# Solving the diagonal blocks of two neighbouring tiles together in the delta-rule stage of a fused transformer kernel, with a new order of stages and 16 buffer slots

## The chip, the cores and the metric

The program runs on one core of a Trainium2 chip. The time is the device time of one execution in microseconds (us); the profile's engines are PE (matrix multiply; PEld its weight loads), DVE, ACT, POOL and SP, which only issues transfers here. The time before is the median of three runs.

## What is computed

Four sub-layers, each followed by a layer norm, on 16 sequences of 1024 tokens of 256 features. The first two (a causal linear attention with an MLP, and a quantised linear layer) and the convolutions in front of the third are phases A and B of the kernel, the fourth (a mixture of experts on the first 1024 tokens) is phase D. The change is in phase C, the delta rule of the third sub-layer and what is made of its output:

```python
def step(S, xs):                       # one chunk, per head
    qi, ki, ui, wi = xs
    attn = jnp.where(tri_lo, qi @ jnp.swapaxes(ki, -1, -2), 0.0)
    u_i = ui - wi @ S
    o = qi @ S + attn @ u_i
    return (S + jnp.swapaxes(ki, -1, -2) @ u_i, o)
...
stats = jnp.concatenate([_stats(local_short), _stats(local_long), _stats(delta_out), _stats(vh)], -1)
...
hgate = jax.nn.gelu(gate_in @ mlp_w1 + mlp_b1, approximate=False)
logits = hgate @ mlp_w2 + mlp_b2
probs = jax.nn.softmax(logits / temp, -1)
...
o = probs[..., 0:1] * local_short + probs[..., 1:2] * local_long + probs[..., 2:3] * delta_out + probs[..., 3:4] * vh
o = o * jax.lax.rsqrt(jnp.mean(o * o, -1, keepdims=True) + 1e-05) * rms_w
return o.reshape(b, l, H * DV) @ Wo
```

There are 4 heads of 64 features; a layer norm and the residual follow.

## The kernel before

Phase C works on 128 tiles of 128 tokens. A "lane" `s` is one of the 16 sequences, `i` one of its 8 tiles; the tiles are taken lane by lane, so that a tile's state `S` comes from 16 tiles earlier. Each tile passes through some 20 stages, which are spread over the engines and pipelined over the tiles. The table `starts` gives for each engine and stage a time within one tile's passage; `interleaved` sorts stage and lane by `s * PERIOD + start`, and this is the order in which each engine issues its stages. The times of the table set the order alone: at run time an engine goes through its own list and waits at semaphores. PERIOD is the table's distance of two tiles. All 128 tiles are written out one after another.

The recurrence inside a tile is solved in 4 blocks of 32 tokens. PE writes `k @ S` and the values into a bank (`kS`); then for each block b ACT takes the 32 rows out as `z`, PE multiplies them with the ready-made 32x32 inverse (`solve{b}`, 4 heads, each a matmul of 32 rows with 64 columns), ACT takes them out as `u`, and PE adds what the solved blocks contribute to the next (`carry{b}`). Block b lies on partitions 32b to 32b+31, for operands and result alike, so a `solve{b}` works in row group b of the array. Neighbouring tiles use two different banks (`CHAIN`). An fp32 matmul shows as two passes in the profile, so a `solve` is 8 passes.

After the blocks PE makes the output (`o`) and the state's increment (`dS`); DVE takes statistics of four sources (`stats`, the longest stage there), POOL takes powers (`l2`, `softmax`), PE runs the gate (`base`, `statsT`, `pre`, `logits`, `turn_logits`), ACT, DVE and POOL mix the sources, PE projects (`oT`, `Wo`), and two layer norms follow (`lnC`, `lnD`), whose variance goes over POOL. DVE and POOL both start their part of `mix` when DVE has signalled `coef_ready`. SP issues the loads of a tile (8 and 3 transfers, `load` and `load_src`) and the store of its result. Each buffer of `slots(...)` exists SLOTS times, or as often as its own number says.

Of the kernel before, what the change touches and what calls it, by code (L numbers as in the profile page):

```python
# [30 lines left out]
CUT = 32  # L31
# [1414 lines left out]
def phase_c(nc, w, k, scratch, out, batches, banks):  # L1446
# [15 lines left out]
    BLOCKS = P // CUT  # L1462
# [2 lines left out]


    starts = {
        "sp": {"load": 0.00, "load_src": 0.51, "lnD": 99.59},
        "pe": {"gram": 5.48, "kS": 6.66, "solve0": 8.45, "carry1": 9.84, "solve1": 11.99, "carry2": 14.89,
               "solve2": 16.30, "carry3": 17.79, "solve3": 20.45, "o": 23.27, "dS": 34.76, "base": 41.20,  # L1470
               "statsT": 48.10, "pre": 51.20, "logits": 55.51, "turn_logits": 59.66, "oT": 76.15, "Wo": 78.51},
        "act": {"kS": 7.84, "solve0": 9.25, "carry1": 11.38, "solve1": 12.79, "carry2": 15.69, "solve2": 17.20,
                "carry3": 18.59, "solve3": 22.47, "o": 26.00, "base": 44.73, "statsT": 48.58, "pre": 52.82,
                "logits": 56.89, "mix": 67.63, "rms": 71.70, "oT": 76.77, "lnC": 94.92, "lnD": 98.78},
        "dve": {"gram": 6.66, "dS": 35.49, "stats": 35.92, "logits": 60.13, "softmax": 66.78, "mix": 67.42,
                "add": 69.04, "rms": 72.39, "Wo": 80.67, "lnC_stats": 81.10, "lnD_stats": 95.84},
        "pool": {"l2": 42.93, "softmax": 62.47, "mix": 67.41, "rms": 73.12, "lnC_stats": 91.17, "lnD_stats": 97.45},
    }
    run = partial(run_pipelined, written=WRITTEN)
    order = {eng: interleaved(own, STEPS, PERIOD) for eng, own in starts.items()}  # L1480
# [3 lines left out]
    CHAINS = 2  # L1484
    CHAIN = [BANKS - C - CHAINS + m for m in range(CHAINS)]
# [12 lines left out]
    with ExitStack() as ctx:  # L1498
        def sb(name, shape):
            return ctx.enter_context(nc.sbuf_tensor("c_" + name, shape, F32))  # L1500

        def slots(name, shape, n=SLOTS):


            own = [sb(f"{name}{m}", shape) for m in range(n)]
            return [own[m % n] for m in range(SLOTS)]

# [3 lines left out]
        psum = [ctx.enter_context(nc.psum_tensor(f"c_bank{b}", [P, BANK], F32)) for b in range(BANKS)]  # L1511
# [23 lines left out]
        z = slots("z", [P, H, DH], 2)  # L1535
# [22 lines left out]
        oT, xs = xT, o_sb  # L1558
# [23 lines left out]
        with nc.Block() as block:  # L1582
# [66 lines left out]
        chain_full, z_ready, u_ready = ([sem(f"{n}{m}") for m in range(CHAINS)] for n in (  # L1649
            "chain_full", "z_ready", "u_ready"))  # L1650
# [220 lines left out]
        def _(dve):  # L1871
# [16 lines left out]
            def stats_stage(i, s):  # L1888

                sl = s % SLOTS  # L1890
                in_sbuf(dve, i, s, "o")
                dve.wait_ge(src_in[s % SRCS], 48 * (uses(i, s, SRCS) + 1))
                for n in range(SRC):
                    for h in range(H):
                        ins = dve.bn_stats(bn[sl][:, n * H + h], src[sl][:, n, h * DH:(h + 1) * DH])  # L1895
                link(ins)
                b = bn[sl][:].rearrange("p (s h) e -> p s h e", s=SRC)
                out_ = stats[sl][:, :, 0].rearrange("p h s e -> p s h e")
                mean, diff, m2, total = (stat[n][:] for n in ("mean", "diff", "m2", "abs"))
# [3 lines left out]
                link(dve.tensor_reduce(total, src[sl][:].rearrange("p s (h d) -> p s h d", h=H), AX.X, ALU.add,  # L1903
                                       apply_absolute_value=True))
# [3 lines left out]
                dve.tensor_scalar(out_[:, :, :, 2], total, 1.0 / DH, None, ALU.mult)  # L1908
                link(dve.scalar_tensor_tensor(m2, diff, DH / 4.0, m2, ALU.mult, ALU.add))
                dve.tensor_scalar(out_[:, :, :, 1], m2, 1.0 / DH, None, ALU.mult)  # L1910
                dve.scalar_tensor_tensor(l2sq[sl][:].rearrange("p (s h) -> p s h", s=SRC), mean, DH / 4.0, m2,  # L1911
                                         ALU.mult, ALU.add).then_inc(N["l2sq_ready"], 1)

            def logits(i, s):
                sl = s % SLOTS
                src_ = full(dve, i, s, "logits")
                ins = dve.scalar_tensor_tensor(logit[sl][:], heads(src_[:, 0:P])[:, :, 0:SRC], inv_temp[:, 0:1],
                                               gate_b2[:, None, :].broadcast_to([P, H, SRC]), ALU.mult, ALU.add)
                done_with(ins, s, "logits")
                in_sbuf(dve, i, s, "logits")  # L1920
                link(dve.tensor_reduce(small[:], logit[sl][:], AX.X, ALU.max))
                dve.tensor_tensor(logit[sl][:], logit[sl][:], small[:, :, None].broadcast_to([P, H, SRC]),  # L1922
                                  ALU.subtract).then_inc(N["logit_ready"], 1)

            def softmax(i, s):
                sl = s % SLOTS
                dve.wait_ge(N["exp_ready"], seq(i, s))
                link(dve.tensor_reduce(small[:], expd[sl][:], AX.X, ALU.add))
                link(dve.reciprocal(small[:], small[:]))
                link(dve.tensor_tensor(coef[sl][:], expd[sl][:], small[:, :, None].broadcast_to([P, H, SRC]), ALU.mult))  # L1930
# [29 lines left out]
            def norm_stats(which, src_, var_sem, ready=None):  # L1960
# [19 lines left out]
        def _(pe):  # L1980
# [25 lines left out]
            def k_state(i, s):  # L2006
# [10 lines left out]
                                    stop=True, skip_group_check=True)  # L2017
                ins.then_inc(chain_full[m], 1)

            def solve(b):  # L2020

                def stage(i, s):
                    m, sl, rows = s % CHAINS, s % SLOTS, slice(b * CUT, (b + 1) * CUT)
                    pe.wait_ge(z_ready[m], BLOCKS * uses(i, s, CHAINS) + b + 1)
                    for h in range(H):
                        ins = pe.matmul(psum[CHAIN[m]][rows, D + h * DH:D + (h + 1) * DH], inverse[sl][rows, h], z[sl][rows, h],  # L2026
                                        start=True, stop=True, skip_group_check=True)
                    ins.then_inc(chain_full[m], 1)
# [305 lines left out]
```

## Time and profile before

| | |
|---|---|
| median of 3 runs | 5204.71 us (5199.36 to 5206.39) |
| profiled execution: its time | 5198.8 us |
| profiled execution: its span, first to last instruction | 5197.0 us |
| mean granted clock | 0.957 |
| PE busy | 4769.5 us (92%) |
| DVE busy | 4121.5 us (79%) |
| ACT busy | 2835.2 us (55%) |
| POOL busy | 2775.8 us (53%) |

Phase C is the part from about 3370 to 5056 us of the span. The busy shares are of the whole span; what an engine has left in phase C must be read from that stretch. All times below are us from the start of the span.

### The profile page before, as it was taken

Reading aid. Unit: us, or ns where it says so; the run is one execution under the profiler, and the core shown is the slowest. Engines: PE = TensorE matmul, PEld = TensorE weight load, DVE = VectorE, ACT = ScalarE, POOL = GpSimd, SP = SyncE. Lnnn points to the kernel's source line nnn. Section 1 sums busy time; section 2 is a strip of 40 time slices with the busy share of each in tenths; the row PEclk is TensorE's granted clock in tenths of the full one; section 3 lists DMA queues with packets and bytes.
Section 4 is the critical chain, followed back from the end, with each engine's and each line's share of the span. In section 5 each row is a group of like instructions: output and inputs, shape, how many; then the busy total and the mean of one; then the engine's idle time right before and its main releaser. Section 6 shows DMA issues by size and latency. Waiting matters only on the chain. (4 is left out here: it accounts for less than half of the span.)

```text
span 5197.0 us, 116254 instructions
## 1 busy us (share of the span) xinstructions
PE 4769.5 (92%) x42012; PEld 3991.7 (77%) x42012; DVE 4121.5 (79%) x12689; ACT 2835.2 (55%) x6469; POOL 2775.8 (53%) x3719
## 2 busy tenths in 40 slices
PE   5999999999999999999999849699999999999968
PEld 4887887878787788778878649678888888888855
DVE  4778988988988898898889842168988889888861
ACT  2554555555455555545555412157777777777751
POOL 1344444444443444444444323248888888888870
PEclk9999999999999999999999969889999999999979
DMA  1121221122122112212121238633433343333320
GB/s 43 42 61 52 63 61 57 53 63 65 50 61 63 54 56 65 64 47 65 57 59 57 61 78 199 165 105 109 115 114 108 114 115 109 112 114 113 110 66 33
DMA packets 738174, 416.01 MB, mean 80 GB/s; under 512 B 341764, under 2 KB 725576, under 8 KB 737608
## 3 DMA queue, kind: packets, MB, share of 16 engines
q1 hardware_dynamic: 667144, 372.92, 25.2%
q10 hardware_dynamic: 65664, 16.78, 1.4%
q0 software_dynamic: 4800, 18.88, 1.2%
q8 instruction: 342, 5.60, 0.5%
q14 instruction: 224, 1.84, 0.1%
HBM read 220.98 MB, written 187.43 MB: 79 GB/s over the span
## 5 line engine op out<-in xcount | busy, mean ns | idle before, releaser
L636 POOL TENSOR_TENSOR a_shift<-a_mean_var,a_eps 128x2 f32<-128x2 f32 x256 | 71.7, 280 | 1423.8 <-DVE a_mean_var L918 1423.8
L932 DVE SCALAR_TENSOR_TENSOR a_cv<-a_raw,a_taps,a_cv 128x256 f32<-128x256 f32 x1152 | 567.2, 565 | 10.1 <-DVE a_scaled L864 9.9
L1151 PE MATMUL a_bank<-a_turned,a_w 128*128 128x256 f32 x2048 | 456.8, 381 | 4.8 <-ACT a_turned L719 4.8
L1053 PE MATMUL a_bank<-a_w,a_hidden 128*128 128x256 f32 x2048 | 452.8, 379 | 0.9 <-ACT a_hidden L764 0.9
L1151 PEld LDWEIGHTS a_bank<-a_turned,a_w 128*128 128x128 f32 x2048 | 384.6, 190 | 59.3 <-ACT a_turned L719 8.8
L1053 PEld LDWEIGHTS a_bank<-a_w,a_hidden 128*128 128x128 f32 x2048 | 384.1, 190 | 51.2 <-ACT a_hidden L764 1.7
L1737 POOL TENSOR_TENSOR c_stats<-c_l2sq,half 128x16 f32<-128x16 f32 x128 | 374.7, 2927 | 57.6 <-DVE c_l2sq L1911 57.6
L1744 POOL TENSOR_TENSOR c_expd<-c_e,c_logit 128x16 f32<-128x16 f32 x128 | 371.3, 2901 | 5.7 <-DVE c_logit L1922 5.7
L897 DVE TENSOR_TENSOR a_masked<-a_bank,keep_causal 128x512 f32<-128x512 f32 x512 | 317.5, 682 | 61.2 <-PE a_bank L1109 59.8
L2026 PE MATMUL c_bank<-c_z,c_inverse 32*32 32x64 f32 x4096 | 323.9, 218 | 4.1 <-ACT c_z L1786 4.0
L2026 PEld LDWEIGHTS c_bank<-c_z,c_inverse 32*32 32x32 f32 x4096 | 241.1, 105 | 72.0 <-issue 20.6
L780 ACT ACTIVATE a_raw<-a_bank 128x512 f32<-128x512 f32 x192 | 114.9, 598 | 301.9 <-PE a_bank L1044 301.9
L667 POOL TENSOR_TENSOR a_coef<-a_base,a_powers_half 128x24 f32<-128x24 f32 x64 | 274.9, 4295 | 5.0
L1895 DVE BATCH_NORM_STATS2 c_bn<-c_src 128x6 f32<-128x64 f32 x2048 | 272.0, 211 | 4.0
L792 ACT ACT_TABLE_LOAD x62 | 79.5, 1283 | 334.5 <-PE a_bank L1171 334.5
L2041 PEld LDWEIGHTS c_bank<-c_u,c_grams 32*32 32x32 f32 (+2 forms) x3072 | 182.6, 107 | 95.3 <-issue 70.0
L982 DVE TENSOR_TENSOR a_T<-a_T,a_product 128x30 f32<-128x30 f32 (+14 forms) x480 | 242.3, 505 | 16.5
L2041 PE MATMUL c_bank<-c_u,c_grams 32*32 32x64 f32 (+2 forms) x3072 | 241.8, 220 | 9.0 <-ACT c_u L1783 4.8
L1786 ACT ACTIVATE c_z<-c_bank 32x256 f32<-32x256 f32 x512 | 191.7, 374 | 93.4 <-PE c_bank L2041 58.9
L1754 POOL TENSOR_TENSOR c_mixed<-c_src,c_coef 128x256 f32<-128x256 f32 x256 | 176.4, 710 | 113.0 <-DVEq L1932 113.0
L1430 PE MATMUL b_bank<-b_window,b_matrix 128*128 128x128 f32 x1024 | 226.0, 397 | 9.7 <-POOL b_window L1322 9.7
L1430 PEld LDWEIGHTS b_bank<-b_window,b_matrix 128*128 128x128 f32 x1024 | 211.5, 211 | 23.1 <-issue 10.2
(291 smaller groups left out, 13254.3 us busy)
## 6 DMA issues: line engine op xcount, KB each, us to landing
a_x<-in_x SPq DMA_DIRECT2D x64, 256.0 KB, 3.0
scratch_xb<-a_xb SPq DMA_DIRECT2D x64, 256.0 KB, 2.1
scratch_xbT<-a_turned SPq DMA_DIRECT2D x128, 128.0 KB, 2.2
scratch_qT<-a_cv SPq DMA_DIRECT2D x128, 128.0 KB, 2.2
scratch_v<-a_qkv_rows SPq DMA_DIRECT2D x64, 256.0 KB, 2.2
scratch_kn<-a_kn SPq DMA_DIRECT2D x64, 256.0 KB, 2.1
scratch_vb<-a_qkv_rows SPq DMA_DIRECT2D x64, 256.0 KB, 2.1
scratch_kT<-a_kT SPq DMA_DIRECT2D x128, 128.0 KB, 2.6
```

The source lines that it names most:

```text
L667: link(pool.tensor_tensor(coef[s][:], base[s][:], powers_half[:], ALU.pow))
L897: ins = dve.tensor_tensor(masked[t][:, r], src[:].rearrange("p (h i) -> p h i", h=C * 2), k["keep_causal"][:, None, :].broadcast_to([P, C ...
L932: ins = dve.scalar_tensor_tensor(cv[s][:, n, c], raw[s][:, n, c, j:j + TOK], taps[:, n, c, j:j + 1], cv[s][:, n, c], ALU.mult, ALU.add)
L982: ins = dve.tensor_tensor(rest, rest, part, ALU.add)
L1053: ins = pe.matmul(dst[:, t * D:(t + 1) * D], src[s][:, c, tile_cols(t)], weight[:, c], start=(c == 0), stop=(c == chunks - 1))
L1151: ins = pe.matmul(dst[:, at:at + TOK], w1_sb[:, c, m * P:(m + 1) * P], x1nT[s][:, c], start=(c == 0), stop=(c == C - 1))
L1430: ins = pe.matmul(dst[:, (c - q * QUAD) * N:(c - q * QUAD + 1) * N], taps_of, window[h][:, :, c], start=True, stop=True)
L1737: pool.tensor_tensor(stats[s % SLOTS][:, :, 0, :, 3], l2sq[s % SLOTS][:].rearrange("p (s h) -> p h s", s=SRC), k["half"][:].rearrange("p ( ...
L1744: pool.tensor_tensor(expd[sl][:], e_base[:].rearrange("p (h e) -> p h e", h=H), logit[sl][:], ALU.pow).then_inc(N["exp_ready"], 1)
L1895: ins = dve.bn_stats(bn[sl][:, n * H + h], src[sl][:, n, h * DH:(h + 1) * DH])
L2026: ins = pe.matmul(psum[CHAIN[m]][rows, D + h * DH:D + (h + 1) * DH], inverse[sl][rows, h], z[sl][rows, h], start=True, stop=True, skip_gro ...
L2041: ins = pe.matmul(psum[CHAIN[m]][rows, h * DH:(h + 1) * DH], grams[sl][known, h % 2, h // 2, 0, rows], u_sb[sl][known, h], start=False, st ...
```

## The change

`solve{b}` for b of 0 and 1 now issues block b of its own tile and block b+2 of the tile before, head by head in turn. `solve2` and `solve3` issue nothing but for the last tile. The table of starts is new, with PERIOD 11.70 in place of 12.90, and DVE's `gram` stands at 6.77 in place of 6.66, and SLOTS is 16 in place of 8 (buffers with a number of their own keep it). DVE's scratch tile `small` is split in two, `largest` and `total`.

```diff
-    SLOTS = 8
-    PERIOD = 12.90
+    SLOTS = 16
+    PERIOD = 11.70
...
-        "pe": {"gram": 5.48, "kS": 6.66, "solve0": 8.45, "carry1": 9.84, "solve1": 11.99, "carry2": 14.89,
...
-        "pool": {"l2": 42.93, "softmax": 62.47, "mix": 67.41, "rms": 73.12, "lnC_stats": 91.17, "lnD_stats": 97.45},
...
+        "pe": {"gram": 5.48, "kS": 6.65, "solve0": 8.93, "carry1": 11.35, "solve1": 13.49, "carry2": 15.69,
...
+        "pool": {"l2": 39.42, "softmax": 68.60, "mix": 78.84, "rms": 94.91, "lnC_stats": 112.54,
+                 "lnD_stats": 120.14},
...
-        small = sb("small", [P, H])
+        largest, total = sb("largest", [P, H]), sb("total", [P, H])
...
+            def solve_one(b, i, s, h):
+
+                m, sl, rows = s % CHAINS, s % SLOTS, slice(b * CUT, (b + 1) * CUT)
+                ins = pe.matmul(psum[CHAIN[m]][rows, D + h * DH:D + (h + 1) * DH], inverse[sl][rows, h], z[sl][rows, h],
+                                start=True, stop=True, skip_group_check=True)
+                if h == H - 1:
+                    ins.then_inc(chain_full[m], 1)
+
             def solve(b):
 
                 def stage(i, s):
-                    m, sl, rows = s % CHAINS, s % SLOTS, slice(b * CUT, (b + 1) * CUT)
-                    pe.wait_ge(z_ready[m], BLOCKS * uses(i, s, CHAINS) + b + 1)
+                    both = [(b, i, s)]
+                    if s > 0:
+                        both.append((b + 2, i, s - 1))
+                    elif i > 0:
+                        both.append((b + 2, i - 1, STEPS - 1))
+                    for b_, i_, s_ in both:
+                        pe.wait_ge(z_ready[s_ % CHAINS], BLOCKS * uses(i_, s_, CHAINS) + b_ + 1)
                     for h in range(H):
-                        ins = pe.matmul(psum[CHAIN[m]][rows, D + h * DH:D + (h + 1) * DH], inverse[sl][rows, h], z[sl][rows, h],
-                                        start=True, stop=True, skip_group_check=True)
-                    ins.then_inc(chain_full[m], 1)
+                        for b_, i_, s_ in both:
+                            solve_one(b_, i_, s_, h)
                 return stage
```

On PE, one tile's period in the middle of phase C, before. `c_z,c_inverse` is a solve, `c_u,c_grams` with 32x64 a carry; x4 are the four heads.

```order
L2001 MATMUL c_bank<-c_qkT 128x256 x4
L2014 MATMUL c_bank<-c_vb,ident 128x256
L2016 MATMUL c_bank<-c_state,c_qkT 128x128 x2
L2026 MATMUL c_bank<-c_z,c_inverse 32x64 x4
L2108 MATMUL c_bank<-ident,c_logitsT 128x128
L2026 MATMUL c_bank<-c_z,c_inverse 32x64 x4
L2063 MATMUL c_bank<-c_u,c_kn 128x128 x2
L2070 MATMUL c_bank<-ident,c_stats 128x128
L2041 MATMUL c_bank<-c_u,c_grams 32x64 x4
L2052 MATMUL c_bank<-c_state,c_qkT 128x128 x2
L2055 MATMUL c_bank<-c_u,c_grams 128x64 x4
```

The same place on PE in the changed kernel, from the same matmuls on:

```order
L2002 MATMUL c_bank<-c_qkT 128x256 x4
L2015 MATMUL c_bank<-c_vb,ident 128x256
L2017 MATMUL c_bank<-c_state,c_qkT 128x128 x2
L2074 MATMUL c_bank<-c_state,c_qkT 128x128 x2
L2077 MATMUL c_bank<-c_u,c_grams 128x64 x4
L2024 MATMUL c_bank<-c_z,c_inverse 32x64 x8
L2085 MATMUL c_bank<-c_u,c_kn 128x128 x2
L2092 MATMUL c_bank<-ident,c_stats 128x128
L2124 MATMUL c_bank<-c_pre,c_gate 32x128 x8
L2136 MATMUL c_bank<-ident,c_on 128x128 x2
L2063 MATMUL c_bank<-c_u,c_grams 32x64 x8
```

The four solves of a period, x4 each, have become two of x8, and the two carries between them stand side by side (x8). `o` (`c_state,c_qkT` and `c_u,c_grams` with 128x64) now stands between `kS` and the solve.

Inside one x8 on PE in the changed kernel, with buffer numbers: bank 4 is the younger tile's (block 0), bank 5 the older one's (block 2).

```order
L2077 MATMUL c_bank1<-c_u0,c_grams0 128x64 x4
L2024 MATMUL c_bank4<-c_z0,c_inverse2 32x64
L2024 MATMUL c_bank5<-c_z1,c_inverse1 32x64
...
L2085 MATMUL c_bank2<-c_u0,c_kn0 128x128 x2
L2063 MATMUL c_bank4<-c_u2,c_grams2 32x64 x4
L2063 MATMUL c_bank5<-c_u1,c_grams1 32x64 x4
```

The two rows in the middle come four times in turn; each tile keeps its bank.

On ACT in the changed kernel, behind the take-out of `z` after `kS`: the square of the mix, `lnC` (which waits for POOL's variance), the output's four heads, and then the two take-outs of `u` that the solve pair left.

```order
L1787 ACTIVATE c_z<-c_bank 32x256
L1815 ACTIVATE c_mixed<-c_o 128x256
L1826 ACTIVATE c_xc<-c_o,c_shift,c_rstd 128x256
L1796 ACTIVATE c_src<-c_bank,c_coef_in 128x64 x4
L1784 ACTIVATE c_u<-c_bank 32x256 x2
L1860 ACTIVATE c_statsT<-c_bank 128x128
L1851 ACTIVATE c_logitsT<-c_bank 128x128
```

The place on ACT before where two take-outs of `u` follow each other, behind the output's norm `lnD` (`c_y`):

```order
L1786 ACTIVATE c_z<-c_bank 32x256
L1825 ACTIVATE c_y<-c_xc,c_shift,c_rstd 128x256
L1783 ACTIVATE c_u<-c_bank 32x256 x2
L1859 ACTIVATE c_statsT<-c_bank 128x128
L1786 ACTIVATE c_z<-c_bank 32x256
L1854 ACTIVATE c_xT<-c_bank,c_rms_w 128x256
```

In both a norm that waits for POOL stands ahead of two take-outs of `u`, for which PE's next carry waits: before it is `lnD`, now `lnC`, and now the output's four heads stand between them too.

## Rows read from the trace of the kernel before

**Rows 1.** The page's head: engines over the whole span.

```profile
PE 4769.5 (92%) x42012; PEld 3991.7 (77%) x42012; DVE 4121.5 (79%) x12689; ACT 2835.2 (55%) x6469; POOL 2775.8 (53%) x3719
```

**Rows 2.** Engines by stretch in phase C; the columns are named in the first line.

```profile
core 0: us, PE busy (x) PEld busy (x) DVE busy (x) ACT busy (x) POOL busy (x), PEclk, DMA share, GB/s
...
4000.00:4200.00 200.00, 199.44 (x2132) 160.71 (x2132) 179.59 (x764) 150.06 (x413) 175.89 (x241) 1.00 0.39 112
```

**Rows 3.** Timeline of PE, one tile's period: start, length, passes.

```profile
4005.86 1.16 PE L2091 MATMUL c_bank<-c_statsT,c_gate_stats 64*128 64x128 f32 x16
4006.95 1.13 PE L2120 MATMUL c_bank<-c_Wo,c_xT 128*128 128x256 f32 x4
...
4008.57 1.16 PE L2078 MATMUL c_bank<-c_xT,c_gate 128*128 128x128 f32 x8
4009.66 0.63 PE L2026 MATMUL c_bank<-c_z,c_inverse 32*32 32x64 f32 x8
4010.22 0.64 PE L2102 MATMUL c_bank<-c_pre,c_gate 128*32 128x128 f32 x16
```

**Rows 4.** Timeline of PE in phase A: four row groups in turn, and blocks of 32 columns.

```profile
2003.69 1.15 PE L1109 MATMUL a_bank<-a_phiq_own,a_phik 32*128 32x256 f32 x16
2023.76 0.76 PE L1200 MATMUL a_bank<-a_kT 64*32 64x32 f32 x64 [0.77 <-ACT a_kT L817]
```

**Rows 5.** Waits of all engines from 3600 to 4800: us in total, times, longest.

```profile
POOL c_mixed L1754 <- DVEq L1932: 82.8, 95, 1.0
DVE c_state L1885 <- PE c_bank L2063: 51.4, 95, 0.6
```

**Rows 6.** All of line 1937: DVE's part of the mix, ns min/median/max.

```profile
L1937 DVE TENSOR_TENSOR c_mixed<-c_src,c_coef x128: 425/892/895, 3442.0 to 5039.4; 128x256 f32<-128x256 f32 x128
```

**Rows 7.** Timeline of DVE in one period.

```profile
4002.92 0.58 DVE L1885 TENSOR_TENSOR c_state<-c_state,c_bank 64x128 f32<-64x128 f32 x2 [0.55 <-PE c_bank L2063]
...
4008.06 0.16 DVE L1928 TENSOR_REDUCE c_small<-c_expd 128x4 f32<-128x16 f32 x1
...
4008.99 0.89 DVE L1937 TENSOR_TENSOR c_mixed<-c_src,c_coef 128x256 f32<-128x256 f32 x1
4009.92 0.42 DVE L1957 TENSOR_TENSOR c_o<-c_bank,c_xb 128x256 f32<-128x256 f32 x1
```

**Rows 8.** Timeline of POOL and ACT in the same period.

```profile
4000.67 0.18 POOL L1729 TENSOR_TENSOR c_shift<-c_mean_var,c_eps 128x1 f32<-128x1 f32 x1
4001.97 0.20 POOL L1761 TENSOR_TENSOR c_o_ssq<-c_o_ssq,c_eps 128x4 f32<-128x4 f32 x1
...
4008.98 1.38 POOL L1754 TENSOR_TENSOR c_mixed<-c_src,c_coef 128x256 f32<-128x256 f32 x2 [0.79 <-DVEq L1932]
4010.32 2.93 POOL L1737 TENSOR_TENSOR c_stats<-c_l2sq,half 128x16 f32<-128x16 f32 x1
...
4002.56 0.76 ACT L1783 ACTIVATE c_u<-c_bank 32x256 f32<-32x256 f32 x2
...
4006.36 0.93 ACT L1795 ACTIVATE c_src<-c_bank,c_coef_in 128x64 f32<-128x64 f32 x4
```

**Rows 9.** Timeline of phase C's start: DVE's first, second and seventh `gram`, one PE carry.

```profile
3380.95 1.29 DVE L1876 TENSOR_TENSOR c_grams<-c_bank,c_keep 128x512 f32<-128x512 f32 x2 [8.67 <-PE c_bank L2001]
...
3384.99 1.03 PE L2041 MATMUL c_bank<-c_u,c_grams 32*32 32x64 f32 x8 [0.55 <-ACT c_u L1783]
...
3394.14 1.29 DVE L1876 TENSOR_TENSOR c_grams<-c_bank,c_keep 128x512 f32<-128x512 f32 x2 [11.91 <-PE c_bank L2001]
...
3457.75 1.29 DVE L1876 TENSOR_TENSOR c_grams<-c_bank,c_keep 128x512 f32<-128x512 f32 x2 [0.29 <-PE c_bank L2001]
```

**Rows 10.** Timeline of DVE at phase C's end, from its last `gram`.

```profile
4983.39 1.25 DVE L1876 TENSOR_TENSOR c_grams<-c_bank,c_keep 128x512 f32<-128x512 f32 x2
...
5027.41 0.17 DVE L1928 TENSOR_REDUCE c_small<-c_expd 128x4 f32<-128x16 f32 x1 [5.67 <-POOL c_expd L1744]
...
5055.07 0.18 DVE L1966 BATCH_NORM_AGGREGATE c_mean_var<-c_bn_ln 128x2 f32<-128x6 f32 x1
```

More of the change, by code:

```diff
@@ L1467, in phase_c @@
     starts = {
-        "sp": {"load": 0.00, "load_src": 0.51, "lnD": 99.59},
-        "pe": {"gram": 5.48, "kS": 6.66, "solve0": 8.45, "carry1": 9.84, "solve1": 11.99, "carry2": 14.89,
[L1470 to L1476, printed above, removed]
-        "pool": {"l2": 42.93, "softmax": 62.47, "mix": 67.41, "rms": 73.12, "lnC_stats": 91.17, "lnD_stats": 97.45},
+        "sp": {"load": 0.00, "load_src": 0.51, "lnD": 122.92},
+        "pe": {"gram": 5.48, "kS": 6.65, "solve0": 8.93, "carry1": 11.35, "solve1": 13.49, "carry2": 15.69,
+               "solve2": 20.63, "carry3": 23.59, "solve3": 25.19, "o": 30.94, "dS": 32.92, "base": 39.60,
+               "statsT": 45.06, "pre": 49.18, "logits": 56.94, "turn_logits": 59.19, "oT": 104.59, "Wo": 106.18},
+        "act": {"kS": 7.83, "solve0": 10.76, "carry1": 12.18, "solve1": 14.30, "carry2": 17.73, "solve2": 22.14,
+                "carry3": 24.38, "solve3": 26.31, "o": 32.79, "base": 41.48, "statsT": 46.18, "pre": 50.79,
+                "logits": 58.08, "mix": 83.23, "rms": 90.07, "oT": 105.21, "lnC": 113.85, "lnD": 122.11},
+        "dve": {"gram": 6.77, "dS": 33.65, "stats": 34.08, "logits": 62.54, "softmax": 78.20, "mix": 78.65,
+                "add": 86.62, "rms": 90.70, "Wo": 111.03, "lnC_stats": 111.38, "lnD_stats": 114.68},
+        "pool": {"l2": 39.42, "softmax": 68.60, "mix": 78.84, "rms": 94.91, "lnC_stats": 112.54,
+                 "lnD_stats": 120.14},
     }
@@ L1898, in stats_stage @@
                 out_ = stats[sl][:, :, 0].rearrange("p h s e -> p s h e")
-                mean, diff, m2, total = (stat[n][:] for n in ("mean", "diff", "m2", "abs"))
+                mean, diff, m2, sizes = (stat[n][:] for n in ("mean", "diff", "m2", "abs"))
                 dve.tensor_tensor(mean, b[:, :, :, 1], b[:, :, :, 4], ALU.add)
@@ L1902, in stats_stage @@
                 dve.tensor_tensor(m2, b[:, :, :, 2], b[:, :, :, 5], ALU.add)
-                link(dve.tensor_reduce(total, src[sl][:].rearrange("p s (h d) -> p s h d", h=H), AX.X, ALU.add,
+                link(dve.tensor_reduce(sizes, src[sl][:].rearrange("p s (h d) -> p s h d", h=H), AX.X, ALU.add,
                                        apply_absolute_value=True))
@@ L1907, in stats_stage @@
                 dve.tensor_tensor(mean, mean, mean, ALU.mult)
-                dve.tensor_scalar(out_[:, :, :, 2], total, 1.0 / DH, None, ALU.mult)
+                dve.tensor_scalar(out_[:, :, :, 2], sizes, 1.0 / DH, None, ALU.mult)
                 link(dve.scalar_tensor_tensor(m2, diff, DH / 4.0, m2, ALU.mult, ALU.add))
@@ L1920, in logits @@
                 in_sbuf(dve, i, s, "logits")
-                link(dve.tensor_reduce(small[:], logit[sl][:], AX.X, ALU.max))
-                dve.tensor_tensor(logit[sl][:], logit[sl][:], small[:, :, None].broadcast_to([P, H, SRC]),
+                link(dve.tensor_reduce(largest[:], logit[sl][:], AX.X, ALU.max))
+                dve.tensor_tensor(logit[sl][:], logit[sl][:], largest[:, :, None].broadcast_to([P, H, SRC]),
                                   ALU.subtract).then_inc(N["logit_ready"], 1)
@@ L1927, in softmax @@
                 dve.wait_ge(N["exp_ready"], seq(i, s))
-                link(dve.tensor_reduce(small[:], expd[sl][:], AX.X, ALU.add))
-                link(dve.reciprocal(small[:], small[:]))
-                link(dve.tensor_tensor(coef[sl][:], expd[sl][:], small[:, :, None].broadcast_to([P, H, SRC]), ALU.mult))
+                link(dve.tensor_reduce(total[:], expd[sl][:], AX.X, ALU.add))
+                link(dve.reciprocal(total[:], total[:]))
+                link(dve.tensor_tensor(coef[sl][:], expd[sl][:], total[:, :, None].broadcast_to([P, H, SRC]), ALU.mult))
                 link(dve.scalar_tensor_tensor(coef[sl][:], coef[sl][:], 1.0 - 2.0 * FLOOR, floor[:], ALU.mult, ALU.add))
@@ L2018, in k_state, with solve_last, stage @@
                 ins.then_inc(chain_full[m], 1)
+            def solve_one(b, i, s, h):
[4 more added lines that the diff above has]
+                    ins.then_inc(chain_full[m], 1)
             def solve(b):
                 def stage(i, s):
-                    m, sl, rows = s % CHAINS, s % SLOTS, slice(b * CUT, (b + 1) * CUT)
-                    pe.wait_ge(z_ready[m], BLOCKS * uses(i, s, CHAINS) + b + 1)
-                    for h in range(H):
-                        ins = pe.matmul(psum[CHAIN[m]][rows, D + h * DH:D + (h + 1) * DH], inverse[sl][rows, h], z[sl][rows, h],
-                                        start=True, stop=True, skip_group_check=True)
-                    ins.then_inc(chain_full[m], 1)
+                    both = [(b, i, s)]
[5 more added lines that the diff above has]
+                        pe.wait_ge(z_ready[s_ % CHAINS], BLOCKS * uses(i_, s_, CHAINS) + b_ + 1)
+                    for h in range(H):
+                        for b_, i_, s_ in both:
+                            solve_one(b_, i_, s_, h)
+                return stage
+            def solve_last(b):
+                def stage(i, s):
+                    if i == TILES - 1 and s == STEPS - 1:
+                        pe.wait_ge(z_ready[s % CHAINS], BLOCKS * uses(i, s, CHAINS) + b + 1)
+                        for h in range(H):
+                            solve_one(b, i, s, h)
                 return stage
@@ L2128, in _ @@
                           stop=True).then_inc(N["pre_opened"], 1)
-            for b in range(BLOCKS):
+            for b in range(2):
                 stages[f"solve{b}"] = solve(b)
+                stages[f"solve{b + 2}"] = solve_last(b + 2)
             for b in range(1, BLOCKS):
```

## The prediction

> **What bounds the kernel now.** I read the page's head first [rows 1]: PE is busy 92% of the whole span, but DVE 79% is an average over phases with other limits. So I went on to the engines by stretch in the middle of phase C [rows 2]: there PE is busy 199.44 of 200 us at the full clock (1.00, the 2.4 GHz level), DVE 90% and POOL 88%. The list of waits over 1200 us of this stretch [rows 5] has no row of PE. PE never waits: phase C goes at PE's pace. The reader is to see in the same list how little the others have left. DVE waits 51.4 us in 95 tiles, 0.54 per tile, always for PE's state increment; POOL waits 82.8 us, 0.87 per tile, always for DVE's `coef_ready`.
>
> The period: DVE's seventh `gram` starts at 3457.75 [rows 9], its last, the 128th, at 4983.39 [rows 10]. 1525.64 us over 121 tiles is 12.61 us per tile. So DVE needs 12.61 - 0.54 = 12.07 us per tile when it waits for nobody, POOL 12.61 - 0.87 = 11.74.
>
> **The solves.** A `solve` of 8 passes takes 4010.22 - 4009.66 = 0.56 us [rows 3], 70 ns a pass, four of them 2.24 us per tile. All passes of one solve use one row group. What alternation of row groups does is seen twice. `pre` (L2091, two halves of 64 rows in turn) issues 16 passes of 128 columns in 1.09 us, 68 ns each; `base` (L2078, all 128 rows), with as many columns, takes 1.09 us for 8, 136 ns each [rows 3]. Half, as two row groups should give. In phase A, 16 passes of 256 columns over four row groups take 1.15 us, 72 ns each [rows 4], where L2120 with all rows takes 1.13 for 4 [rows 3]: a quarter. The pair of solves works in row groups b and b+2, writes different partitions and different banks. So I take half: 35 ns a pass, 0.56 us for the 16 passes of a pair. The bounds are 70 ns (nothing overlaps, 1.12 us) and the 12 ns a pass of L1200's 64 passes in 0.76 us [rows 4] (0.19 us). PE saves 2 x 0.56 = 1.12 us per tile and needs 11.49. The carries, 8 passes each, keep their cost.
>
> A rule of the Trainium skill speaks against this (TensorE: Matmul & The Clock Gate, "Back-to-back issue gap"): with the hardware decoder off, a matmul costs its sequencer about 62 ns however small it is. By it a pair would cost 0.99 us, PE 12.35 and the kernel about 5173 us by the sum below, an estimate; the trace's 12 ns a pass [rows 4] contradicts it for this program.
>
> **Where the gain ends.** PE at 11.49 is faster than DVE at 12.07, so DVE takes over the period: of PE's 1.12 us only 0.54 are worth anything. DVE's instructions are the same ones in another order; splitting `small` changes none of them and removes no semaphore, and 16 slots only relax waits that have no row in [rows 5]. I price both at nothing. If a slot wait had mattered it would stand as a wait on SP's loads ahead of PE's `gram`; the load leads `gram` by 5.5 us in the table before and after.
>
> DVE's part of the mix has a median of 892 ns, a minimum of 425 [rows 6]. It starts with POOL's mix (4008.99 and 4008.98 [rows 7, 8]), because both wait for the same signal. POOL will still get there early: its 11.74 against 12.07 leaves 0.33 us, and all of it lies at that wait. So the 892 stay in DVE's 12.07.
>
> **Does the new order make DVE wait elsewhere?** I lay one period out, zero where DVE ends `stats`. DVE then does `logits`, `add`, `Wo`, `lnC_stats`, `gram`, `softmax` (0.93 us), `mix` (0.93), `rms`, `lnD_stats`, `dS` and `stats` (5.14 from `dS`'s start to `stats`' end) [rows 7]. That leaves 5.07 for the seven short ones; less 1.2 for `gram` and an estimated 1.1 for `rms` and `lnD_stats`, the first four take 2.8. The tightest path: POOL's `l2` 2.9 (start at most 0.3), its `lnC` 1.30 [rows 8] to 4.5; ACT's norm, no longer than the 0.93 of the output, to 5.4; the output 0.93 to 6.4; two `u` 0.76 [rows 8] to 7.1. Behind it on PE wait the two carries and then, up to the end of the next `gram`, an estimated 6.8 of PE's 11.49: 13.9. DVE wants that `gram` at 12.07 + 2.8 = 14.9. One microsecond is to spare. DVE's `stats` wants the output at 7.5 and has it at 6.4. `dS` leaves PE about 3.6 us behind PE's `gram`, and DVE wants it about 4.1 behind its own start of `gram`. No new DVE wait, by some margin.
>
> **Start and end of phase C.** At the start PE goes hop by hop: 1.03 us of passes and about 0.5 waiting for ACT [rows 9]. Between the first two `gram` (13.19 us) lie six hops, in the new order four: 10.2. Later intervals carry both tiles' solves in the same four hops; I take 66 us for the first six against 76.8 before (3457.75 - 3380.95), -11, bounds 0 and -20. At the end, from the last `gram` 71.9 us pass [rows 10]. POOL's last stage stood 7.0 periods behind `gram` in the table and stands 9.7 behind now, so more is still open when the last tile enters. By the tables POOL has one more power of the softmax (2.9), two mixes (1.34), two of `rms` (an estimated 1.9) and five norms (1.3) to do: 16 us. Against that, DVE waits 5.67 us at such a power there, which the new table sets further apart. I take +12, bounds 0 and +24.
>
> **Sum.** 121 x -0.54 = -65; -11; +12: -64. The profiled execution took 5198.8 us, which gives 5135; the median of the runs lies 5.9 above the profiled one, so 5140.
>
> **The rivals.**
> - *DVE's mix escapes POOL's* (0.12). DVE drops towards 12.07 - 0.47 and POOL's 11.74 becomes the period: another 0.33 x 121 = 40, 5100 us. The minimum of 425 [rows 6] shows that it can; the same wait for both engines speaks against it. The Trainium skill (SBUF — State Buffer, "Who interferes with whom") has the two-input DVE instruction and POOL's reads exclude each other, first come first served, so the gain hangs on DVE coming first.
> - *New short waits of DVE*, or solve pairs that overlap only partly (0.13): `gram`, `dS` and the norm are set close behind their sources in the table. 0.25 us a tile costs 30: 5170. The 62 ns rule falls in here; the trace gives it 0.02 of these.
> - *The pair does not overlap* (0.05): PE stays at 12.61 without a gap, start and end cancel: 5205. [rows 3, 4] speak against it.
> - *Slower* (0.09): ACT's `lnC` waits for POOL, and behind it on ACT stand the output and both `u`, for which PE's carries wait. The path above would have to be 1.5 us longer than laid out (1.0 to spare and the 0.54) before the period passes 12.61; 2 us longer gives 13.1 and 121 x 0.46 = 56 more than before: 5260. The path is pinned by POOL, which is busy 11.74 of 12.07, and this speaks for it.
> - *As forecast* (0.61): its own range is 5120 to 5160, from the bounds of start and end and the scatter of the runs.
>
> **How the numbers follow.** The range takes in the forecast, the escape and the short waits, and leaves out no overlap and slower: 5100 to 5180. A measurement of this kernel tells about 0.2% (10 us) from no change. Faster: 0.61 + 0.12 + 0.13 = 0.86; the same: 0.05; slower: 0.09.
>
> **What would show it.** The changed trace should have 16 solve passes in about 0.56 us; a period of 12.1; DVE nearly without waits and about 94% busy there; PE busy about 95%, with gaps that add up to 0.5 us a tile, most likely ahead of the carries; POOL's wait for `coef_ready` down from 0.87 to about 0.3; L1938 (the mix) still at 0.89; the last `gram` to DVE's last instruction about 84 us. Wrong would be: gaps of DVE ended by PE or ACT of over 0.2 us a tile, solve passes at 70 ns, or a POOL that never waits.

## The result, and the profile after

| | before | after |
|---|---|---|
| median | 5204.16 us (4 runs, 5199.36 to 5206.39) | 5130.43 us (4 runs, 5120.81 to 5130.76) |
| ratio | | 0.9855, interval 0.9838 to 0.9872 |
| profiled execution | 5198.8 us, span 5197.0 | 5120.81 us, span 5119.1 |
| mean granted clock | 0.957 | 0.957 |

Forecast were 5140 us, so the miss is 10 us; the profiled execution is the fastest of its four runs. Timed again beside the experiments the same kernel took 5133.65 us. The page's head, against [rows 1]:

```profile
PE 4617.7 (90%) x42012; PEld 3868.0 (76%) x42012; DVE 4119.6 (80%) x12689; ACT 2802.1 (55%) x6469; POOL 2775.1 (54%) x3719
```

PE has the same number of instructions and 152 us less busy time; DVE's and POOL's busy time is what it was, ACT's is 33 us less. The stretch from 4000 to 4200 us, with the columns of [rows 2]:

```profile
4000.00:4200.00 200.00, 189.66 (x2237) 153.22 (x2233) 187.63 (x791) 152.77 (x430) 184.20 (x253) 1.00 0.41 117
```

PE fell from 199.44 to 189.66 of 200 us, DVE rose from 179.59 to 187.63. Which of them binds is told by the waits from 3600 to 4800 us (us in total, times, longest), of which these matter:

```profile
ACT c_xc L1826 <- POOL c_shift L1733: 115.4, 99, 1.2
...
PE c_bank L2063 <- ACT c_u L1784: 45.0, 100, 0.5
...
POOL c_mixed L1755 <- DVEq L1933: 30.8, 99, 0.4
...
PE c_bank L2136 <- ACT c_src L1796: 11.9, 60, 0.2
```

In [rows 5] PE had no row and DVE one of 51.4 us. Now DVE has none, and PE waits 0.45 us a tile ahead of the carries and 0.12 ahead of L2136, which turns `on` for the projection (the stage `oT`): the bound has moved from PE to DVE. DVE's `gram` times, the second, the seventh and the 128th, and the last instruction of DVE in phase C, against [rows 9, 10]:

```profile
3375.34 1.29 DVE L1877 TENSOR_TENSOR c_grams<-c_bank,c_keep 128x512 f32<-128x512 f32 x2 [9.15 <-PE c_bank L2002]
3384.15 1.29 DVE L1877 TENSOR_TENSOR c_grams<-c_bank,c_keep 128x512 f32<-128x512 f32 x2 [7.53 <-PE c_bank L2002]
...
3442.24 1.29 DVE L1877 TENSOR_TENSOR c_grams<-c_bank,c_keep 128x512 f32<-128x512 f32 x2 [0.96 <-PE c_bank L2002]
...
4894.97 1.25 DVE L1877 TENSOR_TENSOR c_grams<-c_bank,c_keep 128x512 f32<-128x512 f32 x2
...
4976.97 0.18 DVE L1967 BATCH_NORM_AGGREGATE c_mean_var<-c_bn_ln 128x2 f32<-128x6 f32 x1
```

The period is (4894.97 - 3442.24) / 121 = 12.01 us against 12.61. On PE's timeline, `kS` (L2017) with `o` (L2074, L2077) right behind it, the solve pair, and the carries that wait:

```profile
4003.96 0.61 PE L2017 MATMUL c_bank<-c_state,c_qkT 128*128 128x128 f32 x4
4004.41 0.61 PE L2074 MATMUL c_bank<-c_state,c_qkT 128*128 128x128 f32 x4
4004.85 1.00 PE L2077 MATMUL c_bank<-c_u,c_grams 128*128 128x64 f32 x8
4005.79 0.64 PE L2024 MATMUL c_bank<-c_z,c_inverse 32*32 32x64 f32 x16
4006.35 0.71 PE L2085 MATMUL c_bank<-c_u,c_kn 128*128 128x128 f32 x4
...
4008.85 1.17 PE L2063 MATMUL c_bank<-c_u,c_grams 32*32 32x64 f32 x16 [0.45 <-ACT c_u L1784]
```

16 passes of the solves take 4006.35 - 4005.79 = 0.56 us, as long as 8 did in [rows 3]. And the mix, against [rows 6]:

```profile
L1938 DVE TENSOR_TENSOR c_mixed<-c_src,c_coef x128: 425/892/896, 3444.4 to 4954.9; 128x256 f32<-128x256 f32 x128
```

### The profile page after: what moved, and what is told of

The parts are those of the page before. It is cut to its first block and busy times, and to the rows that moved or that the text cites. A ratio compares the mean times of both kernels' runs of the same rounds, so it can differ in the third digit from the quotient of the medians.

```text
span 5119.1 us, 116501 instructions
## 1 busy us (share of the span) xinstructions
PE 4617.7 (90%) x42012; PEld 3868.0 (76%) x42012; DVE 4119.6 (80%) x12689; ACT 2802.1 (55%) x6469; POOL 2775.1 (54%) x3719
## 5 line engine op out<-in xcount | busy, mean ns | idle before, releaser
L2063 PE MATMUL c_bank<-c_u,c_grams 128*32 128x64 f32 (+2 forms) x3072 | 232.3, 219 | 57.4 <-ACT c_u L1784 57.3
L2063 PEld LDWEIGHTS c_bank<-c_u,c_grams 128*32 128x32 f32 (+2 forms) x3072 | 182.4, 107 | 111.9 <-issue 83.1
L637 POOL TENSOR_TENSOR a_rstd<-a_shift,neg_half 128x2 f32<-128x2 f32 x256 | 205.3, 802 | 20.0
L1784 ACT ACTIVATE c_u<-c_bank 32x256 f32<-32x256 f32 x512 | 192.1, 375 | 43.1 <-PE c_bank L2024 33.9
L764 ACT ACTIVATE a_hidden<-a_bank,a_b 128x256 f32<-128x256 f32 x512 | 200.3, 480 | 19.1 <-PE a_bank L1151 18.2
```

Source lines behind the costliest of these rows:

```text
L637: link(pool.tensor_tensor(rstd[s][:, which], shift[s][:, which], k["neg_half"][:, 0:T], ALU.pow))
L2063: ins = pe.matmul(psum[CHAIN[m]][rows, h * DH:(h + 1) * DH], grams[sl][known, h % 2, h // 2, 0, rows], u_sb[sl][known, h], start=False, st ...
```

## The experiments

They were timed in three groups, each against the kernel before on the same chip: "The changed kernel again", "Without the turns", "DVE's mix later" and "Less work for DVE" (median of the kernel before 5199.95 us); "Solves apart" and the two in which both places are moved (5201.08, another chip); the last three (5199.84, the chip of the first group). Between groups the ratios are the safer comparison. "Period" is the distance of DVE's `gram` in the middle of phase C, or from the seventh to the 128th where a count of 121 stands with it; the first comes out some 0.02 us longer (12.03 for the changed kernel).

**The changed kernel again**

> The changed kernel once more, as a yardstick on this chip: 5120 to 5131 us, ratio to the kernel before 0.984 to 0.987.

5133.65 us (5128.52 to 5138.04), ratio 0.9872, interval 0.9857 to 0.9887. (4909.29 - 3453.97) / 121 = 12.03. The waits repeat too. The median lies 3 us above the range that I had put; the ratio, 0.9872, is at its edge.

**Without the turns**

```diff
-                    for h in range(H):
-                        for b_, i_, s_ in both:
+                    for b_, i_, s_ in both:
+                        for h in range(H):
                             solve_one(b_, i_, s_, h)
```

> The changed kernel, but the pair of solves is issued one after the other (four heads of one tile, then four of the other) and not head by head in turn. Theory (the turns between two row groups save PE's time, the order by itself nothing): 16 passes take 1.1 us again, PE is the bound at 12.6 us per tile and never waits, and the 121 steady periods cost 0.6 us each more than in the changed kernel: 5195 us, within 8 of the kernel before. Rival (the gain comes from the new order and the cover behind each hop): it stays within 10 us of the changed kernel. Second rival (the weight loads overlap across the border of the two solves alone): between 5160 and 5180.

5137.97 us (5135.47 to 5140.91), ratio 0.9881, interval 0.9866 to 0.9896: 4.3 us above the changed kernel. Timeline of PE, the pair and what follows it:

```profile
4000.57 0.88 PE L2024 MATMUL c_bank<-c_z,c_inverse 32*32 32x64 f32 x16
4001.38 0.71 PE L2085 MATMUL c_bank<-c_u,c_kn 128*128 128x128 f32 x4
```

The pair takes 0.81 us, neither the 1.12 that I expected nor 0.56. Two solves in different row groups take less than twice one solve even when one is issued whole before the other; the turns are worth the remaining 0.25 us a pair. That the row groups are the reason for the first part is not shown: no run has two solves of one row group side by side. PE was busy 1172.17 of 1200 us from 3600 to 4800, at a period of 12.03 that is 11.75 us a tile, still less than DVE's 12.03. So nothing showed in the time. My expectation of 5195 fell. The rival's number (within 10 us of the changed kernel) came out, but not for its reason: PE did lose time, and it was covered by DVE.

**Solves apart**

```diff
-               "solve2": 20.63, "carry3": 23.59, "solve3": 25.19, ...
+               "solve2": 18.80, "carry3": 23.59, "solve3": 25.90, ...
...
-                    if s > 0:
-                        both.append((b + 2, i, s - 1))
-                    elif i > 0:
-                        both.append((b + 2, i - 1, STEPS - 1))
```

(`solve2` and `solve3` issue their own block for every tile.)

> The changed kernel, but each solve is issued by itself: solve2 of the older tile before o (table 18.80 instead of 20.63), solve3 behind pre (25.90 instead of 25.19), so that six and eight other matmuls lie between it and the younger tile's solve. A solve of 8 passes in one row group took 0.56 us in the kernel before. Theory A (two solves save PE time only where they stand next to each other): PE needs 11.49 + 2 x 0.56 = 12.6 a tile, period 12.6, time 5200 us, like the kernel before. Theory B (a solve overlaps the matmuls of another kind around it just as well): PE needs 12.0 or less, DVE goes on binding, 5135 us. Between them: a new wait in the chain of blocks would show as PE idle ahead of a solve with ACT as releaser.

5194.89 us (5183.13 to 5198.16), ratio 0.9984, interval 0.9974 to 0.9993. The stretch from 3600 to 4800, columns as in [rows 2], and one of the four solves with what stands around it:

```profile
3600.00:4800.00 1200.00, 1200.00 (x12817) 969.01 (x12816) 1101.22 (x4591) 892.90 (x2486) 1061.70 (x1438) 1.00 0.40 113
```

```profile
4007.65 0.61 PE L2017 MATMUL c_bank<-c_state,c_qkT 128*128 128x128 f32 x4
4008.19 0.63 PE L2024 MATMUL c_bank<-c_z,c_inverse 32*32 32x64 f32 x8
4008.75 0.71 PE L2069 MATMUL c_bank<-c_state,c_qkT 128*128 128x128 f32 x4
4009.30 1.00 PE L2072 MATMUL c_bank<-c_u,c_grams 128*128 128x64 f32 x8
```

PE is busy without a gap, each solve takes 0.56 us again, the period is 12.54. In this order, without the pairing, the new table and the 16 slots are worth 0.16%. Beside matmuls of another kind a solve gains nothing (theory A).

The edit did one thing more than take the pairs apart: it put a solve between `kS` (L2017) and `o` (L2069, which is L2074 in the changed kernel). There the two take 0.54 and 0.55 us from start to next start, against 0.45 and 0.44 side by side in the changed kernel. So 0.2 us of PE's loss a tile comes from there. An order with four single solves that leaves `kS` and `o` together was not run; by these rows PE would need an estimated 12.34 in it, and the order alone could then be worth up to 0.27 of the 0.60 us a tile. The pairing brings the rest.

**DVE's mix later**

```diff
-        "dve": {... "softmax": 78.20, "mix": 78.65,
+        "dve": {... "softmax": 78.20, "mix": 86.30,
```

> The changed kernel with one number of DVE's table changed: its part of the mix goes from 78.65 to 86.30, behind the next period's logits and just ahead of add, so that it no longer starts together with POOL's mix. Theory (the 892 ns are a collision with POOL's wide reads, 425 ns without it, and DVE is the bound): the mix takes 0.43 us, DVE needs 11.54 us per tile, POOL's own mix loses up to 0.14 us too, and the period becomes POOL's or PE's, 11.6 to 11.75: 5085 us with 5075 to 5100. Rival (the 892 ns belong to the instruction after softmax, or DVE collides with another of POOL's instructions where it now stands): same time as the changed kernel. Second rival (PE's chain over ACT, which waited for POOL, binds before that): 5105 to 5115.

5135.05 us (5128.81 to 5143.52), ratio 0.9879, interval 0.986 to 0.9897: no change. Lines 1938 and 1906 (a product of 16 columns in `stats`), ns min/median/max, and the two engines' timelines at one place:

```profile
L1938 DVE TENSOR_TENSOR c_mixed<-c_src,c_coef x128: 393/449/455, 3464.8 to 4972.8; 128x256 f32<-128x256 f32 x128
L1906 DVE TENSOR_TENSOR c_stat_diff<-c_stat_diff x128: 175/607/610, 3417.4 to 4939.9; 128x16 f32<-128x16 f32 x128
```

```profile
4002.01 0.61 POOL L1765 TENSOR_TENSOR c_on<-c_o,c_o_inv 128x256 f32<-128x256 f32 x1
...
4002.05 0.60 DVE L1906 TENSOR_TENSOR c_stat_diff<-c_stat_diff 128x16 f32<-128x16 f32 x1
```

The 892 ns went, and a product that took 175 ns took 607: it now starts 0.04 us behind POOL's `c_on` and ends with it. DVE still has no wait, and the period stays at 12.01. The first rival held: DVE lost on one instruction what it gained on another.

**Less work for DVE**

```diff
-    ... tensor_reduce(sizes, src[sl][:].rearrange("p s (h d) -> p s h d", h=H), AX.X, ALU.add,
+    ... tensor_reduce(sizes, src[sl][:].rearrange("p s (h d) -> p s h d", h=H)[:, :, :, 0:16], AX.X, ALU.add,
```

> The changed kernel with less work on DVE: the sum of absolute values goes over 16 of each 64 columns, so that this statistic is left out for three quarters of its input; 1.21 us become about 0.4. Theory (DVE is the bound at 12.01): the period falls to POOL's 11.74 and no further, POOL stops waiting for the coefficients: 121 x 0.27 = 33 us less than the changed kernel, 5090 to 5098. Rival (PE over ACT's take-outs of u is the bound and DVE only follows): no change, 5120 to 5130.

5142.51 us (5136.21 to 5145.86), ratio 0.9888, interval 0.9873 to 0.9903. With 0.8 us less work for DVE the kernel is not faster but 9 us above the changed one, at the edge of what the intervals tell apart; the period in mid-phase is 12.09 against 12.03. POOL, which needed 11.74 before, now never waits, and DVE waits 0.24 us a tile for PE's `gram`:

```profile
DVE c_grams L1877 <- PE c_bank L2002: 24.1, 100, 0.3
```

Two of POOL's products of one column, early and late in a period, and DVE beside the late ones, from the timeline:

```profile
4004.07 0.19 POOL L1732 TENSOR_TENSOR c_shift<-c_mean_var,c_rstd 128x1 f32<-128x1 f32 x1
...
4011.21 0.69 DVE L1946 TENSOR_TENSOR c_mixed<-c_mixed 128x512 f32<-128x512 f32 x1
...
4011.37 0.57 POOL L1732 TENSOR_TENSOR c_shift<-c_mean_var,c_rstd 128x1 f32<-128x1 f32 x1
...
4011.93 0.42 DVE L1947 TENSOR_TENSOR c_o<-c_mixed 128x256 f32<-128x256 f32 x1
...
4012.02 0.38 POOL L1733 TENSOR_TENSOR c_shift<-c_shift,c_minus_one 128x1 f32<-128x1 f32 x1
```

The first of POOL's late products ends, at 4011.94, with DVE's 512-wide one, the second with its 256-wide one. The holding up goes both ways. My 5090 to 5098 had taken POOL's 11.74 as its own work, and it isn't fixed.

DVE did not keep its 0.8 us either. With POOL late, DVE's mix came first and took 426 ns (median) in place of 892, the escape of the prediction's first rival. But two products of DVE with a constant fell under POOL's wide ones: L1954 has a median of 545 ns against 194 in the changed kernel, L1911 one of 580 against 181. The first of them, from the timelines:

```profile
4004.47 1.20 POOL L1755 TENSOR_TENSOR c_mixed<-c_src,c_coef 128x256 f32<-128x256 f32 x2
...
4004.63 0.49 DVE L1954 TENSOR_SCALAR c_o_ssq<-c_o_ssq 128x4 f32<-128x4 f32 x1
```

**Both places moved**

```diff
-        "dve": {... "mix": 78.65,
+        "dve": {... "mix": 86.30,
-        "pool": {"l2": 39.42, "softmax": 68.60, "mix": 78.84, "rms": 94.91, ...
+        "pool": {"l2": 39.42, "softmax": 68.60, "mix": 78.84, "rms": 91.40, ...
```

> The changed kernel with two numbers of the table moved: DVE's own mix at 86.30 instead of 78.65, and POOL's rms at 91.40 instead of 94.91, so that POOL's 256-wide product c_on (0.61 us) falls under DVE's statistics of single sources instead of under a short product of DVE. Theory A (each 256-wide POOL product holds up whatever DVE instruction with two SBUF operands, or a dependent short one, meets it, 0.43 to 0.47 us a tile; DVE binds at 12.01): L1938 0.45 and L1906 0.18 us, DVE needs 11.55 a tile, PE with 11.49 and POOL with some 11.6 take over, period 11.6, time 5080 to 5095 us. Theory B (DVE and POOL share something whose sum is fixed, so that the time lost only moves to another instruction): another DVE or POOL instruction grows by 0.4 us, period 12.0, time 5135 us. Theory C (the loop of waits between DVE's coefficients and POOL binds, not DVE's work): DVE's busy time falls but waits take its place, period 12.0, 5135 us.

5094.9 us (5087.0 to 5098.15), ratio 0.9794, interval 0.9779 to 0.9808: the fastest version that leaves nothing out, 39 us under the changed kernel (0.78% by the ratios). The timelines at the place where `c_on` now runs, and the waits of DVE, POOL and PE from 3600 to 4800:

```profile
4010.34 2.13 DVE L1896 BATCH_NORM_STATS2 c_bn<-c_src 128x6 f32<-128x64 f32 x16
...
4011.08 0.61 POOL L1765 TENSOR_TENSOR c_on<-c_o,c_o_inv 128x256 f32<-128x256 f32 x1
```

```profile
PE c_bank L2063 <- ACT c_u L1784: 44.2, 103, 0.5
...
DVE c_o_ssq L1953 <- DVE c_coef L1932: 0.5, 1, 0.5
POOL c_mixed L1755 <- DVEq L1933: 0.5, 1, 0.5
```

The statistics, with one SBUF operand each, lie under `c_on` and stay at 211 ns. The period is (4873.06 - 3458.19) / 121 = 11.69. Theory A holds; B and C fell. DVE and POOL both have no wait (but for one of 0.5 us each), and PE's is 0.43 us a tile. The period is 0.1 above the 11.6 that I had put, and the time at the upper end of my range. A little of the gain was lost elsewhere: against the changed kernel DVE's L1946 rose from 683 to 736 ns (means), POOL's L1733 from 197 to 259.

**Both places moved, without the turns** (the edit of "Without the turns" on top)

> The kernel before this one in the call (DVE's mix at 86.30, POOL's rms at 91.40), with the pair of solves issued four heads of one tile, then four of the other. If PE is the bound once DVE is free of the collisions, its 0.25 us a pair, two pairs a tile, comes back in full: PE needs 11.99 a tile, period 12.0, time about 50 us above that of the version with turns, 5135 us. If POOL or a loop of waits binds at 11.8 or more, the two stand within 25 us. If the period is 12.0 in the other kernel too, no difference.

5109.67 us (5104.33 to 5113.35), ratio 0.9824, interval 0.9809 to 0.9838: 15 us above the kernel with turns. The stretch from 3600 to 4800:

```profile
3600.00:4800.00 1200.00, 1194.97 (x13616) 976.34 (x13612) 1122.69 (x4879) 932.21 (x2644) 1134.03 (x1522) 1.00 0.42 120
```

PE is busy 99.6% at a period of 11.82, so it needs 11.77, as in "Without the turns"; with turns it needs 11.70 - 0.43 = 11.27. The difference is the two times 0.25 us. Only 0.12 of it shows in the period, for at 11.70 the other two bind. That PE alone binds here is not shown: DVE and POOL have no wait in this kernel either, and POOL's L1733 takes 0.14 us a tile more than with turns. I had put PE's need at 11.99, 0.2 too high, and the time 25 us too high.

**Both moved, POOL without its two sign changes; DVE with less work; and both**

```diff
-                    link(pool.tensor_tensor(shift[sl][:, one], mean_var[sl][:, which, 0:1], rstd[sl][:, one], ALU.mult))
-                    pool.tensor_tensor(shift[sl][:, one], shift[sl][:, one], minus[:, 0:1], ALU.mult).then_inc(rstd_sem, 1)
+                    pool.tensor_tensor(shift[sl][:, one], mean_var[sl][:, which, 0:1], rstd[sl][:, one],
+                                       ALU.mult).then_inc(rstd_sem, 1)
```

(POOL's edit; DVE's is that of "Less work for DVE".)

> The version with DVE's mix at 86.30 and POOL's rms at 91.40 (period 11.70; DVE and POOL both show no wait in it), in which POOL leaves out the multiplication by minus one in both layer norms (the bias keeps the wrong sign): two instructions of 0.19 to 0.33 us and their starts, some 0.55 us of POOL a tile. If POOL alone binds: period 11.3, where PE's 11.27 stands, time 5045 us. If DVE binds too: 11.6, L1755 shows POOL waiting for DVE's coefficients again, 0.4 us a tile, time 5080 to 5095 us, the same as without the edit within 15 us.

> The version with DVE's mix at 86.30 and POOL's rms at 91.40, in which DVE's sum of absolute values leaves out 48 of 64 columns (0.8 us of DVE a tile). If POOL binds beside DVE (no wait of either in the version itself): period stays at 11.7, DVE gets waits of up to 0.8 us a tile, time within 15 us of 5095. If only DVE binds: PE's 11.27 or so, time 5045 us. Should the shifted places make a 256-wide product of POOL meet a product of DVE again, an instruction of DVE grows to 0.4 or 0.6 us and DVE's waits are smaller by that.

> Both omissions of the two kernels before it in the call. With DVE at 10.8 and POOL at 11.2 of work a tile PE's own work is what is left: 11.27 (11.70 less the 0.43 that it waited for u in the version with only the table moved). If PE can reach it: period 11.3, time 5045 us. If the chain through ACT and the carry binds (PE waits 0.4 us ahead of the carries whatever the rest does): period stays at 11.6 to 11.7, time 5080 to 5095 us, and that wait stays at 0.4 us a tile.

| | us | ratio, interval | period |
|---|---|---|---|
| POOL less | 5067.13 | 0.9745, 0.9729 to 0.9762 | 11.53 |
| DVE less | 5140.23 | 0.9887, 0.9872 to 0.9902 | 12.09 |
| both | 5054.89 | 0.972, 0.9705 to 0.9734 | 11.38 |

The first waits are those with POOL less, the others those with DVE less:

```profile
POOL c_mixed L1755 <- DVEq L1933: 41.4, 104, 0.9
```

```profile
DVE c_bn_ln L1966 <- ACT c_xc L1826: 89.3, 99, 0.9
```

With POOL less, DVE has no wait and sets 11.53; 5067 lies between my two cases: DVE binds, as in the second, but its need is 11.53 and not the 11.6 that I had put. Nothing of DVE's own work was changed, and yet its need fell from 11.70 to 11.53: it depends on what it meets, as POOL's does. With DVE less, DVE waits 0.9 us a tile for the norm (and 0.24 for PE's `gram`) and POOL sets 12.09, 0.4 more than in the same version with all of DVE's work. My "within 15 us of 5095" missed by 45 us. The timeline of POOL and DVE there shows the piece that grew and its cause:

```profile
4002.40 0.69 DVE L1946 TENSOR_TENSOR c_mixed<-c_mixed 128x512 f32<-128x512 f32 x1
...
4002.53 0.61 POOL L1732 TENSOR_TENSOR c_shift<-c_mean_var,c_rstd 128x1 f32<-128x1 f32 x1
...
4003.13 0.42 DVE L1947 TENSOR_TENSOR c_o<-c_mixed 128x256 f32<-128x256 f32 x1
...
4003.22 0.38 POOL L1733 TENSOR_TENSOR c_shift<-c_shift,c_minus_one 128x1 f32<-128x1 f32 x1
```

Two products of 0.19 us have become 0.61 and 0.38, together 0.61 more. The version before it already had the second at 0.33, so 0.47 of it is new, against 0.37 of period (12.09 against 11.71, both in mid-phase). With both omissions PE is busy 1187.90 of 1200 us, 11.27 us a tile: its own need, as worked out from "Both places moved". The chain through ACT does not bind: PE waits for `u` 1.9 us in all of the stretch. The time is 10 us above the 5045 that I had put, and the period 0.1 above PE's need. POOL has no wait here either: its L1732 takes 417 ns in the mean against 190 with POOL less alone, so by the same reading POOL's need is 11.38, just above PE's.

## Why the prediction was right

**PE bound the kernel before, and the pair halves.** Forecast 0.56 us for 16 passes, measured 0.56. PE's need was forecast at 11.49; the changed kernel's PE is busy 1136.46 of 1200 us at 12.02, which is 11.38 (stalls too short for the list of waits are in it), and "Both places moved" has 11.27. The 0.22 below the forecast is a term that I did not have: `kS` and `o`, now side by side, take 0.2 us less. Putting the solves apart gave PE 12.54 and all but 6 us of the time of before. That the pairing brings time is shown by it; how the gain divides between the pairing and the place of `o` is open, as said there.

The rule of the Trainium skill that I had set against it (TensorE: Matmul & The Clock Gate, "Back-to-back issue gap", 62 ns a matmul with the hardware decoder off) would, counted by passes, have made the pair 0.99 us; the trace has 35 ns a pass. I should have counted matmuls: a pair has 8, the rule then gives 0.50 us, and the pair's 0.56 says nothing against it. What does is L1200 [rows 4]: 64 passes, which are 32 matmuls in the kernel, in 0.76 us are 24 ns a matmul. So the rule doesn't describe this program; whether the decoder is off here no run shows.

**The upper bound of 1.12 us rested on a wrong reason.** I had tied the overlap to the alternation of row groups. Issued one after the other, the pair still took 0.81. So of the 1.12 us that the pairs save PE, about 0.6 us a tile comes from the two solves standing side by side, and 0.5 from the turns. The time doesn't show the second part in the changed kernel, where PE has that much to spare.

**DVE takes over at 12.07.** Measured 12.01, without a row of DVE in the waits. That DVE binds is shown by "Both places moved": PE's work stayed, DVE lost 0.5 us in its mix and the period fell to 11.69. Forecast -65 us for 121 tiles, measured 1452.73 - 1525.64 = -72.9. The term was mis-sized by 0.06 us a tile; which instructions of DVE make it up the traces don't settle.

**The mix stays at 892 ns, POOL's wait falls to 0.33.** Measured 892 and 30.8 / 99 = 0.31.

**No new wait of DVE.** Right; PE's `gram` ends at 4003.49 and DVE's starts at 4004.62 in the period shown, 1.1 us later, where I had 1.0 to spare. And ACT's wait for POOL ahead of `lnC` (115.4 us in 99 tiles, 1.2 each) harmed only PE. The gaps forecast ahead of the carries are there: 0.45 us, and 0.12 at L2136, where 0.5 in all was expected.

**Start and end.** From the first `gram` to the seventh 66.9 us (forecast 66), 9.9 less than before (11). From the last `gram` to DVE's end 82.2 (forecast 84), 10.3 more (12). Phase C also began 5.6 us earlier than in the trace of before, which no part of the change touches. -72.9 - 9.9 + 10.3 - 5.6 = -78.1, and the spans differ by 77.9. The 5.6 are chance: in "The changed kernel again" phase C began 5.9 us later than in the trace of before (3386.82 against 3380.95), the other terms are -70.3, -9.7 and +10.4, and the span is 63.4 us shorter. That this meets the forecast's -64 so closely is luck: the period gave 5 us more than forecast, and the late start took them back. The sizes of the start and the end were rough estimates with wide bounds; that both came out within 2 us is partly luck too.

**The rivals.** No overlap and slower are out. The escape of the mix, which I priced at DVE 11.60 and POOL 11.74 and 5100 us, did not happen in the changed kernel. Made to happen by DVE's table alone it brought nothing, because another product of DVE then met one of POOL's, and the same when it happened by itself in "Less work for DVE"; only with both engines' places set did it give 11.70 and 5095. The price was nearly right, its condition was not complete: the mix had to escape and nothing else be caught.

## What to carry to other kernels

Two sets of small matmuls in different row groups, issued in turn, took PE no longer than one (0.56 us), and one behind the other 0.81; look for such sets in neighbouring tiles. Look also at which matmuls stand beside each other: `kS` and `o` took 0.2 us less together than with a solve between them. When PE is relieved, its gain ends at the next engine, here after half of it. That engine's need is its period less its waits, but as it runs in this kernel: the need of DVE and of POOL moved by 0.2 to 0.4 us with what they met. If DVE and POOL are both over 90% busy, lay their timelines beside each other before shortening either: which wide product of one meets which instruction of the other decided 40 us here, and taking 0.8 us of DVE's work away made the best version 45 us slower.

## What the runs showed of the hardware that was not expected

A product on DVE with two SBUF operands and a POOL product hold each other up until the one that came first has ended: 175 ns became 607 on DVE, 0.19 us became 0.61 on POOL. DVE's statistics and reductions never grew (means of 211 to 213 ns, and 1.21 us wherever they were whole). The Trainium skill (SBUF — State Buffer, "Who interferes with whom") says that the two-input form takes a shared port exclusively and that who issues first decides; both directions in these traces agree. Its list lets a `tensor_scalar` in a two-port mode meet POOL as well, and L1911, a `tensor_scalar` with 16 columns, took 0.58 us under `c_on` in "Less work for DVE" against 0.18 in the changed kernel; that fits, though L1912 with its two operands stands right behind it. L1954 is clearer: a `tensor_scalar` with 4 columns and a one-operand statistic behind it, it took 0.49 us there, to the end of the first of POOL's two mix products (4004.47 + 0.62, the mean of L1755). So it was the `tensor_scalar` that was held up. Whether it ran in a two-port mode no trace shows.

That two solves issued one after the other take less than twice one (0.81 us for 16 passes, 51 ns each, where one alone goes at 70) was not expected either; with turns it is 35. And `kS` and `o`, which use all 128 rows, take 0.45 and 0.44 us side by side and 0.54 and 0.55 with a solve between them. So what stands next to a matmul changes its cost even without separate row groups; why, these runs don't show.
